# A deeper software pipeline in the edge stage of a graph-attention layer

## The reference

```
h = relu(layernorm(x))
q, k, v = h @ wq + bq, h @ wk + bk, h @ wv + bv
scores = sum(q[dst] * k[src], -1) / 16 + edge_weight * we + be
p = exp(scores - segment_max(scores, dst)[dst])
out = segment_sum(v[src] * p[:, None], dst) / segment_sum(p, dst)
y = layernorm(h + out + h @ ws + bs) * g1 + b1
result = x + layernorm(y + gelu(y @ w1 + b1f) @ w2 + b2f) * g2 + b2
```

## Time and profile before

| | |
|---|---|
| Time, median of 3 runs | 2334.37 us (2331.2 to 2334.62) |
| Span of the profiled execution | 3211.3 us |
| Own time of the profiled execution beside that span | not given with this profile |
| Profiled: TensorE, VectorE, ScalarE busy | 76%, 55%, 37% |
| Profiled: GpSimd busy | 51% |
| Mean granted clock of TensorE | 0.921 |

### The profile page before, as it was taken

How to read it: one execution, slowest core, us unless ns; L and a number is a source line. 1 busy time by engine, 2 the same in 40 slices (tenths; PEclk the granted TensorE clock), 3 DMA queues, 4 the chain that set the end, 5 groups by cost and what they waited for, 6 DMA issues and landing times. The chain is left out here.

```text
span 3211.3 us, 68474 instructions
## 1 busy us (share of the span) xinstructions
PE 2427.3 (76%) x14747; PEld 1996.1 (62%) x14748; DVE 1767.6 (55%) x7372; ACT 1193.2 (37%) x2930; POOL 1635.5 (51%) x1828
## 2 busy tenths in 40 slices
PE   7577677777777777777777777777777777778998
PEld 5455556556555556565656566665666666657897
DVE  7454455555555545554555555555555555556787
ACT  6333333333333333333333333333333333334666
POOL 5355565555555545555554555555555445441154
PEclk8898899899899989998998999899988899999999
DMA  7233333333233323333233333332333233222222
GB/s 231 76 103 103 99 105 101 103 98 107 90 100 100 96 86 101 97 98 96 90 102 92 96 90 96 96 98 87 96 96 100 87 92 95 83 93 71 82 74 68
DMA packets 148148, 311.29 MB, mean 97 GB/s; under 512 B 33566, under 2 KB 84625, under 8 KB 148104
## 3 DMA queue, kind: packets, MB, share of 16 engines
q0 software_dynamic: 75264, 205.62, 21.5%
q1 hardware_dynamic: 54718, 90.19, 8.6%
q10 hardware_dynamic: 18122, 14.96, 1.5%
HBM read 290.21 MB, written 20.43 MB: 97 GB/s over the span
## 5 line engine op out<-in xcount | busy, mean ns | idle before, releaser
L488 POOL DMA_INDIRECT work<-h_rows,idx x1536 | 1457.3, 949 | 1339.9 <-SPq L372 956.2
L1079 PE MATMUL bank<-work 128*128 x3520 | 939.0, 412 | 24.5 <-issue 17.7
L1011 PE MATMUL bank<-q,onehot 128*128 x5304 | 804.6, 291 | 1.2 <-DVE work L832 0.7
L1079 PEld LDWEIGHTS bank<-work 128*128 128x128 f32 x3520 | 700.1, 211 | 146.8 <-issue 45.2
L886 DVE CUSTOM_DVE_ANT_0 work<-bank,work 128x512 f32<-128x512 f32 x440 | 330.5, 751 | 778.7 <-remote 476.4
L622 ACT COPY work<-bank 128x256 f32<-128x256 f32 x880 | 295.0, 376 | 1182.6 <-remote 812.8
L832 DVE SCALAR_TENSOR_TENSOR work<-bank,work 128x257 bf16<-128x257 f32 x1764 | 651.6, 425 | 143.5 <-PE bank L1011 44.2
L1017 PE MATMUL bank<-ident,work 128*128 128x128 f32 x1764 | 307.4, 302 | 500.5 <-ACT work L622 313.3
L1011 PEld LDWEIGHTS bank<-q,onehot 128*128 128x128 bf16 x5304 | 549.5, 104 | 85.4 <-issue 1.7
L1017 PEld LDWEIGHTS bank<-ident,work 128*128 128x128 f32 x1764 | 212.8, 148 | 578.0 <-ACT work L622 442.4
L1066 PE MATMUL bank<-ident,work 128*128 128x128 f32 x1760 | 283.6, 285 | 191.8 <-ACT work L619 182.8
(11 more groups left out here) (195 smaller groups left out, 1519.5 us busy)
## 6 DMA issues: line engine op xcount, KB each, us to landing
dst_words<-dst_short SPq DMA_DIRECT2D x99, 512.0 KB
work<-h_rows,idx POOLq DMA_INDIRECT x1568
bias<-h_rows ACTq DMA_DIRECT2D x56, 128.0 KB
r_rows<-bias ACTq DMA_DIRECT2D x55, 128.0 KB
work<-r_rows SPq DMA_DIRECT2D x49, 128.0 KB, 2.3
h_rows<-acc SPq DMA_DIRECT2D x12, 512.0 KB, 6.6
work<-in_x SPq DMA_DIRECT2D x12, 512.0 KB, 3.5
out<-work SPq DMA_DIRECT2D x48, 128.0 KB, 1.7
```

What stands on the lines that cost most here:

```text
L488: pool.indirect_dma_start(rows[:, u, j, 0:D], None, h_rows, bass.IndirectOffsetOnAxis(idx[:, half, u * J + j:u * J + j + 1], 0)).then_inc( ...
L1011: last = nc.tensor.matmul(banks[j][:, 0:D1], onehot[:, k, j, :], q3[:, bass.ds(b, 1), c, 0:D1], start=(c == 0), stop=(c == 2))
L1079: last = nc.tensor.matmul(banks[6 + k][:, 0:D1], probs[:, j, :], rows[:, bass.ds(slot, 1), j, :], start=(j == 2), stop=(j == 1))
```

## The change

A step's work is spread over one more iteration, and there are two buffers where there was one.

- TensorE, iteration s: spread(s+1), third and fourth group of sum(s-1), turn(s), expand(s+3) in two halves, first and second group of sum(s-1). It spreads as soon as masked(s) has read bank 4. All of step s's turned weights go to bank 5, and bank 4 is for spread scores alone. The very first sum is of zeros; the last one is made behind the loop.
- VectorE, iteration s: masked(s), the scores of step s+2 (was s+1), the one-hot of s+4 (was s+3), the sums of s-2 (was s-1). Ahead of the loop it makes the scores and one-hot of one step more.
- ScalarE: the weights are copied in one instruction of 512 columns instead of two of 256, after `prepare` and after the copies of the residual rows (`copy_hTe`, `copy_r`), which are in halves now, from columns behind the sums in banks 6 and 7.
- `masked`, `probs` and `decay` have two (four) buffers; `products` are separate tiles.
- The step table holds block and chunk in other bits, with fewer register instructions for the slot and place on VectorE; bounds of loaded values are made by a mask (`not_below_zero`). `dotted` and `q_edges` are counted by half. The wait for `outside_done` ahead of masked goes.
- `free_tab` asks for one step more before a slot is free. GpSimd's gathers themselves, their number, size and slots, are unchanged.

The core of the diff:

```diff
-        masked = part(C)
+        masked = part(2 * C).rearrange("p (k n) -> p k n", k=2)
         probsT = masked
-        probs = part(C).rearrange("p (j n) -> p j n", j=J)
-        product = part(J * (D1 + 1) // 2, BF16).rearrange("p (j n) -> p j n", j=J)
+        probs_even = part(C).rearrange("p (j n) -> p j n", j=J)
+        products = [part((D1 + 1) // 2, BF16)] + [norms[:, k * (D1 + 1) // 2:(k + 1) * (D1 + 1) // 2].bitcast(BF16) for k in range(J - 1)]
...
+        probs_odd = part(C).rearrange("p (j n) -> p j n", j=J)
+        probs = [probs_even, probs_odd]
...
+        def not_below_zero(eng, loaded, min_val, max_val):
+
+            mask = (1 << max_val.bit_length()) - 1
+            return eng.snap(eng.to_reg(eng.snap(loaded) & mask), min_val=min_val, max_val=max_val)
...
-            return eng.snap(eng.to_reg(step & (BLOCKS - 1)), min_val=0, max_val=B)
+            return eng.snap(eng.to_reg(step >> CHUNK_BITS), min_val=0, max_val=B)
...
-                        nc.scalar.activation(decay[:, k:k + 1], old_max[:, k:k + 1], ACT.Exp, bias=new_max, scale=-1.0)
-                        nc.scalar.activation(probsT, masked, ACT.Exp, bias=new_max, scale=-1.0).then_inc(exp_done, 1)
-                        for half in (1, 0):
-                            act.wait_ge(turned, s * 2 + (2 - half))
-                            nc.scalar.copy(probs[:, 2 * half:2 * half + 2, :].rearrange("p j n -> p (j n)"), banks[5 - half][:, 0:2 * P]).then_inc(probs_done, 1)
+                        nc.scalar.activation(decay[:, u % 4:u % 4 + 1], old_max[:, k:k + 1], ACT.Exp, bias=new_max, scale=-1.0)
+                        nc.scalar.activation(probsT[:, k, :], masked[:, k, :], ACT.Exp, bias=new_max, scale=-1.0).then_inc(exp_done, 1)
                         prepare(s + 2, k)
-                        for at, body in ((3, copy_hTe), (6, copy_r), (7, store_r)):
-                            if steps == U and u == at:
-                                body(act.snap(act.to_reg(r * NW + i), min_val=0, max_val=B * NW))
+                        if steps == U and u in (2, 3):
+                            copy_hTe(act.snap(act.to_reg(r * NW + i), min_val=0, max_val=B * NW), u - 2)
+                        if steps == U and u in (5, 6):
+                            copy_r(act.snap(act.to_reg(r * NW + i), min_val=0, max_val=B * NW), 6 - u)
+                        act.wait_ge(turned, s + 1)
+                        nc.scalar.copy(probs[k][:].rearrange("p j n -> p (j n)"), banks[5][:]).then_inc(probs_done, 1)
+                        if steps == U and u == 7:
+                            store_r(act.snap(act.to_reg(r * NW + i), min_val=0, max_val=B * NW))
...
-                        nc.vector.tensor_scalar(free_row[0:1, 0:most], free_row[0:1, 0:most], float(S - 1), is_sorted[0:1, 0:1], ALU.add, ALU.mult).then_inc(plan, 1)
+                        nc.vector.scalar_tensor_tensor(out=free_row[0:1, 0:most], in0=srow[0:1, 0:most], scalar=float(S), in1=free_row[0:1, 0:most], op0=ALU.is_ge, op1=ALU.add).then_inc(plan, 1)
                         dve.wait_ge(plan, 12)
-                        nc.vector.scalar_tensor_tensor(out=free_tab[0:1, :], in0=free_row[0:1, 0:most], scalar=1.0, in1=srow[0:1, 0:most], op0=ALU.add, op1=ALU.add).then_inc(plan_done, 1)
+                        nc.vector.tensor_scalar(free_row[0:1, 0:most], free_row[0:1, 0:most], float(S - 2), is_sorted[0:1, 0:1], ALU.add, ALU.mult).then_inc(plan, 1)
+                        dve.wait_ge(plan, 13)
+                        nc.vector.scalar_tensor_tensor(out=free_tab[0:1, :], in0=free_row[0:1, 0:most], scalar=2.0, in1=srow[0:1, 0:most], op0=ALU.add, op1=ALU.add).then_inc(plan_done, 1)
...
+                nc.vector.memset(probs[1], 0.0).then_inc(probs_done, 1)
+                edge_scores(ahead[0], 0, 1, 0)
                 dve.wait_ge(outside_done, 1)
                 mark(place_of_mark(ahead[2]), 0)
+                edge_scores(ahead[1], 0, 2, 1)
+                dve.wait_ge(outside_done, 2)
+                mark(place_of_mark(ahead[3]), 1)
...
-                        dve.wait_ge(outside_done, step)
                         dve.wait_ge(max_read, step)
-                        nc.vector.tensor_tensor_reduce(out=masked, in0=banks[4][:], in1=outside[:, k, :], scale=-1.0, scalar=old_max[:, k:k + 1],
+                        nc.vector.tensor_tensor_reduce(out=masked[:, k, :], in0=banks[4][:], in1=outside[:, k, :], scale=-1.0, scalar=old_max[:, k:k + 1],
                                                        op0=ALU.add, op1=ALU.min, accum_out=new_max).then_inc(masked_done, 1)
-                        edge_scores(step_at(regs[u + 1]), r, s + 1, 1 - k, meanwhile)
+                        edge_scores(step_at(regs[u + 2]), r, prepared, k, meanwhile)
...
+                        mark(place[0], k)
                         read_max(s + 1, 1 - k, block_at(u + 1))
-                        add_sums(s, 1 - k, dve.snap(held, min_val=0, max_val=B) if u == 0 else blocks[u - 1])
-                    dve.reg_mov(held, dve.to_reg(blocks[steps - 1]))
+                        if steps == U and u in (2, 3):
+                            dve.wait_ge(hTe_copied, dve.to_reg((r * NW + i) * 2 + (u - 1)))
+                        if steps == U and u in (5, 6):
+                            dve.wait_ge(r_copied, dve.to_reg((r * NW + i) * 2 + (u - 2)))
+                        add_sums(s, u + 2, dve.snap(held[u], min_val=0, max_val=B) if u < 2 else blocks[u - 2])
...
+                def turn_probs(k):
+
+                    for j in range(J):
+                        last = nc.tensor.transpose(banks[5][:, j * P:(j + 1) * P], probsT[:, k, j * P:(j + 1) * P], ident[:])
+                    last.then_inc(turned, 1)
+
+                def sum_rows(k, half, slot):
+
+                    for j in (2 * half, 2 * half + 1):
+                        last = nc.tensor.matmul(banks[6 + k][:, 0:D1], probs[k][:, j, :], rows[:, bass.ds(slot, 1), j, :], start=(j == 2), stop=(j == 1))
+                    if half == 0:
+                        last.then_inc(summed, 1)
...
-                        b, slot = block_of(pe, step_of[u + 2]), slot_of(pe, step_of[u] >> (BLOCKS.bit_length() - 1))
+                        b = block_of(pe, step_of[u + 3])
+                        pe.wait_ge(masked_done, s + 1)
+                        pe.wait_ge(scored, s + 2)
+                        spread_scores(1 - k)
+                        pe.wait_ge(probs_done, s + 1)
+                        sum_rows(1 - k, 1, slot)
                         pe.wait_ge(exp_done, s + 1)
-                        for half in (1, 0):
-                            for j in range(2):
-                                last = nc.tensor.transpose(banks[5 - half][:, j * P:(j + 1) * P], probsT[:, (2 * half + j) * P:(2 * half + j + 1) * P], ident[:])
-                            last.then_inc(turned, 1)
-                        pe.wait_ge(onehot_done, s + (S + 3))
-                        pe.wait_ge(dotted, s * 2 + 3)
-                        expand_q(k, 0, b)
-                        pe.wait_ge(scored, s + 2)
-                        pe.wait_ge(probs_done, s * 2 + 1)
-                        spread_scores(1 - k)
-                        pe.wait_ge(dotted, s * 2 + 4)
-                        expand_q(k, 1, b)
-                        for j in (2, 3, 0, 1):
-                            if j == 0:
-                                pe.wait_ge(probs_done, s * 2 + 2)
-                            last = nc.tensor.matmul(banks[6 + k][:, 0:D1], probs[:, j, :], rows[:, bass.ds(slot, 1), j, :], start=(j == 2), stop=(j == 1))
-                        last.then_inc(summed, 1)
-                        if steps == U and u == 2:
-                            turn_h(pe.snap(pe.to_reg(r * NW + i), min_val=0, max_val=B * NW))
-                        if steps == U and u == 5:
-                            project_h(pe.snap(pe.to_reg(r * NW + i), min_val=0, max_val=B * NW))
+                        turn_probs(k)
+                        pe.wait_ge(onehot_done, s + (S + 4))
+                        pe.wait_ge(dotted[0], s + 3)
+                        expand_q(1 - k, 0, b)
+                        pe.wait_ge(dotted[1], s + 3)
+                        expand_q(1 - k, 1, b)
+                        sum_rows(1 - k, 0, slot)
+                        slot = slot_of(pe, step_of[u])
+                        if steps == U and u in (1, 2):
+                            turn_h(pe.snap(pe.to_reg(r * NW + i), min_val=0, max_val=B * NW), u - 1)
+                        if steps == U and u in (4, 5):
+                            project_h(pe.snap(pe.to_reg(r * NW + i), min_val=0, max_val=B * NW), 5 - u)
...
+                pe.wait_ge(probs_done, all_steps)
+                pe.wait_ge(identity_added, 1)
+                pe.wait_ge(added, all_steps)
+                slot = pe.snap(slot_before, min_val=0, max_val=S - 1)
+                sum_rows(1, 1, slot)
+                sum_rows(1, 0, slot)
```

(60 more changed lines are left out.)

144 lines of the change are left out of this document (75 added, 69 removed).

## The result

The changed kernel takes 2345.23 us (median, 2344.49 to 2346.23). The kernel before took 2334.49 in the same comparison (2331.20 to 2337.04). The ratio is 1.0045, 95% interval 1.0032 to 1.0058: 10.7 us slower.

What follows compares the result with a forecast made beforehand. Unprofiled, GpSimd issuing gathers without a pause was taken as the bound. Start 4.8 plus end 4, other terms 0, gave 8.8 us late, taken as +7: 2334 + 7 = 2341 us, range 2255 to 2360.

Steps and rivals of the forecast that it cites:

- floor of 2346: Whole kernel: time if GpSimd issues gathers without a pause, 150.5 + 1922 + 4 + 295 - 25, 12 us above the median.
- item 1: Hand-overs from TensorE to ScalarE and VectorE: added slack priced at 0, bounds a loss of 0 and a gain of 123 us.
- Rival 1: Edge loop: late signals also in the timed run, GpSimd issuing faster than 1.25 us; 2220 to 2325 us, chance 0.25.
- Item 2: TensorE's work: same matmuls in other order, 4.10 us a step stays, so 0; the zero sum adds 1.90 once.
- Item 3: ScalarE's weight copies: one of 512 for two of 256, hidden, so 0; uncovered, at most a few tenths us a step.
- Item 4: VectorE's shorter loop: fewer register instructions, hidden under TensorE and GpSimd, so 0; bound 0 to 123 us.
- Item 5: VectorE's added waits for ScalarE's copies ahead of four `add_sums` a trip: 0; 81 us if each held.
- Item 6: Start: more work before the first mask and a later first sum delay the first gather 4.8 us; bounds 2 and 7.
- Item 7: End: last chunk's scores made two iterations ahead of its mask, behind all gathers: 4 us; bounds 0 and 5.
- Item 8: Gather slots: each is held longer, but SyncE's existing condition on later gathers is met no earlier, so 0.
- The absorption: Last third of the loop: gathers and TensorE tie, so part of the fill may be absorbed; 8.8 us late taken as +7.
- Rival 3: VectorE and gathers: added waits (81 us) or gathers stretched by each mark (142 us); 2350 to 2480 us, chance 0.09.

Runs made afterwards that it cites:

- e10: Old pipeline with the new register handling, two of each chunk's four indirect gathers replaced by GpSimd plain loads, against the kernel before: 2204.51 us, ratio 0.9447.
- e9: Old pipeline with the new register handling, every gather index the partition's own number, against the kernel before: 2332.21 us, ratio 0.9990.
- e7: Old pipeline with the new register handling, SyncE issuing plain loads in place of all indirect gathers, against the kernel before: 2212.43 us, ratio 0.6897.
- e1: Old pipeline with only the new register handling, against the kernel before: 3205.28 us against 3203.73, ratio 1.0009.
- e5: The changed kernel without edit, against the kernel before on a chip where that is slow: 3069.26 us against 3210.41, ratio 0.9555.
- e8: The changed kernel with SyncE issuing plain loads in place of all indirect gathers, against the kernel before: 2228.64 us, ratio 0.6950.
- e12: Old pipeline with only the new register handling, run once more on another chip, against the kernel before: 3212.36 us against 3210.47, ratio 1.0003.
- e11: The changed kernel with two of each chunk's four indirect gathers replaced by GpSimd plain loads, against the kernel before: 2251.81 us, ratio 0.7012.
- e2: Old pipeline with the new register handling, only 3 of a chunk's 4 gathers in the loop, against the kernel before: 2647.86 us, ratio 0.8265.
- e3: The changed kernel with only 3 of a chunk's 4 gathers in the loop, against the kernel before: 2599.58 us, ratio 0.8117.
- e6: Old pipeline with the new register handling, GpSimd issuing plain loads in place of the loop's indirect gathers, against the kernel before: 2234.86 us, ratio 0.6967.

## Why the prediction was right, and where it was not

Forecast 2341, measured 2345.2: the sign is right, and so are the reason chosen (GpSimd sets the pace, so the fill and the end are paid) and, within what single traces can tell, the start. The increase was forecast at 7 us and is 10.7 by the times, 14.3 by one pair of traces. Point by point:

- **The choice of GpSimd's issue as the bound of the timed run** was right, shown by e10 and by the gathers of e9 and after, 0.95 long with 0.30 between. The Trainium skill's rule for the issuing engine (Perfetto Trace Analysis, What "DMA-bound" means), read on a trace of a quick chip, agrees with this: GpSimd's track there is gather after gather. By its busy share, 70%, it would be missed.
- **The floor of 2346** had right gathers and wrong ends. e9 has 120.5 + 1930.7 + 278.2 = 2329.3. The set-up was taken 30 us too long, from the late-signal chip, and the gathers and tail 13 too short: among others, some four masked steps were left behind the last gather (16.2 us), where two were assumed. The sum came near by luck. The same with TensorE's floor of 2211: e7's span is 2211.3, from a set-up 22 us shorter and steps of 4.165 us, not 4.10 (24 us longer); the five masks of the earlier trace rows don't take in the head of a trip, where the masks of e7 are 4.74 apart and not 3.95. On the quick chip e10 has 2202.6. Even so, at some 130 us apart, the two floors were told apart rightly.
- **The step that failed**, though the forecast held, is the one that sets "the unprofiled time" against the profile: the 877 us between span and median were put down to profiling. e1 and e5 show spans equal to the timed run less 2 us; it is the chip, or its condition. "Fixed durations" fails too: a matmul of the row sums takes 412 ns on average before and 380 in after, at granted clocks of 0.92 and 1.00 in the loop. Two things follow. The span of after was forecast at 2400 to 2950 and is 2343.6. And item 1, slack at 0, is right for the quick chip, but 141 us on a late-signal one (e5). Rival 1's mechanism is real, on other chips than the one of the result.
- **Item 2, TensorE 0**: the groups keep their counts but for the zero sum (8 records) and one expansion more ahead of the loop (12 records, 1.5 us), which item 2 didn't have. Yet e8 against e7 shows 0.27 us a trip more, over half of it a longer stand at the head of the trip. On the quick chip this hides under the gathers (+0.4 between the first and the last).
- **Item 3, ScalarE 0**: one copy of 512 takes 0.59 and two of 256 took 0.37 each; ScalarE is 49% busy and nothing moved.
- **Item 4, VectorE's loop 0**: e1 and e12, 1.0009 and 1.0003, both on late-signal chips; on the quick one e9 bounds it, at 0.9990.
- **Item 5, added waits 0**: right. The trace shows no wait of VectorE for those copies, and the loop has no room for 81 us.
- **Item 6, start +4.8**: measured +6.6 between e9 and after, +6.3 between e10 and after, and +3.8 to +4.8 in the pairs on late-signal chips (e12 and e11, e1 and e5, e2 and e3). What the change itself does is +2.6 ahead of the first mask (2.2 was counted) and, in the way to step 0's sum, +3.2 where the old pipeline starts at the upper clock and +1.5 where it doesn't (2.6 was counted): 4.1 to 5.8. Mechanism and size are right.
- **Item 7, end +4**: measured +7.3, above its bound of 5; this term was mis-sized. The extra iteration is 5.4, and the last sum, which stands alone behind the loop, 1.9. Item 2 has one sum more, of 1.90, but the forecast's sum leaves it out; it shows here. That the last sum is the 1.9 is read off its length.
- **Item 8, slots 0**: right within 0.4.
- **The absorption**, which brought 8.8 down to 7, doesn't show. After's gathers lose only some 6 us over the loop, and e9's as much, so nothing was regained. 6.6 + 7.3 + 0.4 = 14.3 against e9, 10.7 against the kernel before. The 3.6 between them isn't settled. The start at the lower clock, which e9 lacks and e10 has, would make 1.6 of it.

Rival 3's stretched gathers are out: 0.950 us a gather in after, 0.950 in e9, 0.949 before.

## What to carry to other kernels

If a profiled span and the median disagree by more than a few us, first ask whether they are of the same chip; a profile of one can show waits that the other hasn't. Compare traces of a start over more than one run before putting a difference of 2 us down to a change. Build the floor of each engine from its own instructions, the gaps between them included: a GpSimd that is 70% busy can be the bound. A deeper pipeline costs its fill and drain in full where something outside it sets the pace, and earned only where hand-overs were late (141 us in e5); with TensorE as the bound it cost 16 us (e8 against e7); here the next gain lies in fewer or cheaper indirect issues (130 us), not in the order. No run here computes the reference and beats both; gathers that fetch more rows for one issue weren't tried.

## What the runs showed of the hardware

- The same kernel takes 2334 us on some chips and 3204 to 3210 on two others, at a granted clock of 0.99 and 0.92. The longer time comes with waits of ScalarE and VectorE of up to 9.4 us, which end up to some 8 us behind the recorded end of TensorE's work (before, e1, e5). Why some chips do this is open.
- There, the time climbs steeply from the third indirect gather of a chunk on: for the new pipeline 2228.6 with none, 2253.6 with two a chunk, 2599.6 with three, 3069.3 with four. From the first to the last mask it is 1840, 1840, 2184 and 2666 us: two a chunk cost the loop nothing, and the 25 us between the first two runs lie in the set-up (first mask at 123.1 and 149.6), where only the second has 32 indirect gathers. Plain loads of the same bytes cause none of it.
- An indirect gather of 128 rows, one behind the other, holds GpSimd for 0.95 + 0.30 us, with the edges' indices (after) as with each partition's own number (e9); a plain load of 128 rows 0.54 (0.61 between gathers, in e10).
- The granted clock behind the same short stand of TensorE fell to 0.50 in some traces (e1, e2, e10, e12) and stayed at 1.00 in others (before, e6, e9).
